# Attention in an audio tower: the order in which a head's six query tiles are worked, 0, 5, 1, 4, 2, 3 in place of 0, 4, 1, 5, 2, 3

## The reference, cut to what matters

```python
q = jnp.einsum('bqd,hdm->bqhm', x, W_Q) + b_Q          # the same for k and v
scores = jnp.einsum('bqhm,bkhm->bhqk', q, k) / jnp.sqrt(jnp.asarray(D_HEAD, q.dtype))
scores = jnp.where(causal[None, None, :, :], scores, jnp.asarray(IGNORE, scores.dtype))
pattern = jax.nn.softmax(scores, axis=-1)
z = jnp.einsum('bhqk,bkhm->bqhm', pattern, v)
attn_out = jnp.einsum('bqhm,hmd->bqd', z, W_O) + b_O
```

## Time and profile before

| | |
|---|---|
| median of 3 runs | 1612.37 us (1612.15, 1612.37, 1617.33) |
| profiled execution, its own time | 1609.28 us |
| its span | 1607.5 us |
| busy: PE, PEld | 88%, 61% |
| busy: DVE, ACT, POOL | 66%, 48%, 25% |
| mean granted clock of TensorE | 0.938 of full |

### The profile page before, as it was taken

How to read it: one execution, slowest core, us unless ns; L and a number is a source line. 1 busy time by engine, 2 the same in 40 slices (tenths; PEclk the granted TensorE clock), 3 DMA queues, 4 the chain that set the end, 5 groups by cost and what they waited for, 6 DMA issues and landing times.

```text
span 1607.5 us, 29299 instructions
## 1 busy us (share of the span) xinstructions
PE 1416.6 (88%) x10191; PEld 978.7 (61%) x10192; DVE 1068.1 (66%) x2482; ACT 778.8 (48%) x1490; POOL 408.2 (25%) x425
## 2 busy tenths in 40 slices
PE   5987799998987799998987799999886899969997
PEld 3333378886433488884443588883433788856665
DVE  4988655557987555568896555659886555664553
ACT  1664355643654456525563565616643666532332
POOL 3000044513000244403000334302000576721222
PEclk8899899998998899997989999989998999979999
DMA  5997033210000122201000223200000643222221
GB/s 135 344 352 247 1 73 74 53 36 31 12 1 0 39 69 50 69 12 42 1 1 1 58 56 73 50 1 30 1 1 1 156 120 87 52 68 55 64 61 32
DMA packets 109553, 104.81 MB, mean 65 GB/s; under 512 B 51772, under 2 KB 99961, under 8 KB 109425
## 3 DMA queue, kind: packets, MB, share of 16 engines
q1 hardware_dynamic: 80210, 54.53, 14.1%
q10 hardware_dynamic: 25744, 39.62, 7.5%
q0 software_dynamic: 3472, 8.97, 1.6%
HBM read 28.78 MB, written 47.40 MB: 47 GB/s over the span
## 4 chain that ended last, share of the span: by engine, by line
PE 49%; DVE 28%; issue 10%; POOL 5%; ACT 4%; DMA 2%; SPq 2%; POOLq 0%; DVEq 0%; ACTq 0%
PE ps L1879 12%; DVE arena L1301 10%; PE ps L1929 8%; PE ps L1859 7%; DVE arena L1299 6%; PE ps L1869 6%; DVE bn L1458 4%; PE ps L1812 4%; PE ps L1973 3%; PE ps L1818 2%; DMA arena<-arena 2%; SPq L573 1%; POOL out L900 1%; ACT arena L1002 1%; POOL arena L797 1%
## 5 line engine op out<-in xcount | busy, mean ns | idle before, releaser
L1929 PE MATMUL ps<-arena,cwt 128*128 128x504 f16 (+2 forms) x1776 | 391.6, 381 | 40.8 <-DVE arena L1299 38.7
L1929 PEld LDWEIGHTS ps<-arena,cwt 128*128 128x128 f16 x1776 | 175.5, 102 | 257.1 <-DVE arena L1299 42.3
L1320 DVE TENSOR_REDUCE nmax<-ps 128x1 f32<-128x128 f32 (+5 forms) x288 | 173.5, 615 | 116.6 <-PE ps L1862 116.6
L1879 PE MATMUL ps<-arena 128*128 128x64 f32 (+2 forms) x2016 | 237.8, 270 | 2.6 <-DVE arena L1328 2.6
L1879 PEld LDWEIGHTS ps<-arena 128*128 128x128 f32 (+2 forms) x2016 | 229.9, 188 | 8.3 <-DVE arena L1328 4.2
L1301 DVE TENSOR_TENSOR arena<-arena 128x1008 f16<-128x1008 f32 (+4 forms) x200 | 227.1, 1136 | 6.9
L980 ACT ACTIVATE arena<-ps,nmax 128x128 f32<-128x128 f32 (+5 forms) x288 | 181.2, 630 | 58.9 <-DVE nmax L1320 56.3
L1328 DVE COPY arena<-ps 128x512 f32<-128x512 f32 (+4 forms) x288 | 152.1, 535 | 70.0 <-PE ps L1869 67.0
L1042 ACT ACTIVATE arena<-ps 128x1008 f32<-128x1008 f32 (+1 forms) x112 | 96.1, 866 | 179.8 <-PE ps L1929 179.8
L1859 PE MATMUL ps<-arena 128*128 128x512 f16 (+6 forms) x780 | 154.5, 310 | 19.2 <-DMA arena<-arena 10.4
L786 POOL TENSOR_TENSOR tmp<-tmp,neg_half 128x1 f32<-128x1 f32 x24 | 13.3, 553 | 545.4 <-DVE tmp L1202 545.4
(11 more groups left out here) (291 smaller groups left out, 2242.6 us busy)
## 6 DMA issues: line engine op xcount, KB each, us to landing
slot_scratch<-empty_slot ACTq DMA_DIRECT2D x1, 38692.5 KB, 119.9
arena<-arena SPq DMA_DIRECT2D x96, 187.5 KB, 3.0
arena<-arena SPq DMA_DIRECT2D x96, 93.8 KB, 2.4
arena<-in_L_ffn_w SPq DMA_DIRECT2D x16, 288.0 KB, 6.7
arena<-in_L_ffn_w SPq DMA_DIRECT2D x8, 576.0 KB, 7.5
arena<-slot_scratch SPq DMA_DIRECT2D x31, 96.5 KB, 1.9
arena<-slot_scratch SPq DMA_DIRECT2D x31, 96.0 KB, 1.9
xa<-in_x POOLq DMA_DIRECT2D x4, 468.8 KB, 4.7
```

Of the source, the lines that this page charges most:

```text
L1320: v.reduce_max(nmax[0:m, k:k + 1], banks_at(("S", p, k))[0:m, 0:128 * i + m], AX.X, negate=True).then_inc(S["smax_done"], 1)
L1879: last = t.matmul(bank_at(BANKS[job][0])[0:m, 0:DH], probt[(STEPS * p + k) % PROBTS][0:kk, c, 0:m], vt[0:kk, c, DH * hh:DH * hh + DH], sta ...
L1929: last = t.matmul(bank(g, k)[:, 0:c * PITCH].rearrange("p (r c) -> p r c", c=PITCH), cwt[layer][:, w, tap, :], parts[x][:, f:f + 2 * c - 1 ...
```

## The change

One constant differs. Step 1 (and 7 of the second head) works on tile 5 and step 3 (and 9) on tile 4, where it was the other way round. The three lists of steps, the sizes in PSUM banks (both tiles take two) and all waits between steps stay as they were.

```diff
-TILE_ORDER = (0, 4, 1, 5, 2, 3)
+TILE_ORDER = (0, 5, 1, 4, 2, 3)
 STEPS = 2 * TT
```

## The result

The changed kernel took 1626.47 us in the median of 5 runs (1618.69 to 1626.69). Five runs of the kernel before, made beside them, had a median of 1613.47 us (1612.15 to 1617.33). The ratio is 1.0061 with a 95% interval of 1.0034 to 1.0089. The prediction was 1614.8 us with a range of 1611.0 to 1618.5, and it gave a slowdown of over 0.3% a chance of 0.14.

What follows compares the result with a forecast made beforehand. PE bounds the half from S12 to Q, the stack's DMA the half from Q to S12. Per recording 0.21 + 0.24 + 0.16 = 0.61 us, four times +2.4: 1612.37 to 1614.8 us, range 1611.0 to 1618.5.

Steps and rivals of the forecast that it cites:

- S9's gain: Score step between Q and S12, 0.11 us shorter; in middle pairs it only lengthens S12's DMA wait, 0.28 to about 0.37.
- The rival in which all cancels: S12's wait is an issue delay following PE, so S9's gain counts: +0.7 us in all, 1613.1; chance 0.13.
- the waits of Q and Z3: Q's wait in the first pair about 1.5 us, from 1.33; Z3's in the last about 0.9, from 0.65.
- signs of being wrong: Middle-pair period below 24.84 us or up over 0.15; low clock appearing after first-pair Q or vanishing after S2.
- The rule on the share of the weight loads: Loads busy 3.23 of 4.00 us, so PE has spare time; middle halves cost nothing, sum +1.5 us.
- S12 to Q: Half of a middle pair bound by PE itself: +0.06 us each, four per recording, +0.24 us.
- PT2's wait for EX2: Rival: longer CA1 delays EX2, PT2 waits; up to 0.08 us in each of 24 pairs, +1.9, 1616.7; chance 0.10.
- The margin of 0.12 us for PT2: With S3 0.11 us shorter, PT2 comes up at 235.19, still 0.12 us after EX2's end at 235.07.
- First pair: Path to Q's wait for EX7 through S3, PT1, S7, MX7 and EX7: +0.21 us, bounds +0.10 and +0.25.
- Last pair: No Q or K, so Z3 waits for CP3 and S9's gain counts: +0.16 us per recording.
- The rival of the slow clock: Q's longer first-pair wait brings low clock, 1.7 us per recording hit; all four +9.2, 1621.6; chance 0.08.
- Nothing outside the attention changes, it is shifted: Stages outside the attention only move in time; no cost was added for them.

Runs made afterwards that it cites:

- K split: High part of K sent to the stacks as soon as made, low part when ready: old order 1609.73 us (0.9979), new order 1614.06 us (0.9983).
- the unneeded matmuls before S2: 8 dummy matmuls in the wait before S2 of each recording's first pair: old order 1610.13 us (0.9964), new order 1613.31 us (0.9972).
- the new order with both: Changed kernel plus K split and the unneeded matmuls before S2: 1610.39 us, ratio 0.9966 to the kernel before.
- the old with both: Kernel before plus K split and the unneeded matmuls before S2: 1608.99 us, ratio 0.9948.
- the shifted kernel: Kernel before, old tile order, plus twelve dummy matmuls between ZT and the output projections of each recording: 1623.38 us, ratio 1.0044.

## Why the prediction was wrong, point by point

**The waits held as a mechanism.** A pair is a loop of two halves. S12 waited for the stack's DMA: its matmul started 135 ns behind the last landing in each of the 20 handovers of every kernel with that transfer, its load's wait went to 0.36 us, Q to S12 stayed at 12.80, and the split of the transfer let S9's gain come out. The rival in which all cancels is ruled out by this: middle pairs cost 0.10 us each. All three signs were right, and the waits of Q and Z3 moved as said. None of the signs of being wrong that the prediction named came up (the median period grew by 0.09 us, less than its 0.15); they all watched the attention, and a good third of the loss lies behind it.

The rule on the share of the weight loads that the prediction took from the Trainium skill (Perfetto Trace Analysis, Identifying the Most-Contended Engine), by which middle pairs would have cost nothing, is not borne out by the traces here.

**The terms were too small.** S12 to Q: forecast +0.06, measured +0.10. Of this 0.05 is PT2's wait for EX2, which had a chance of 0.10 as a rival at up to 0.08. The step that failed there was "EX2 waits for MX2 at that time, not for CA1": that was so before (MX2 to EX2 0.10 us), but the row after shows EX2 right behind CA1. The margin of 0.12 us for PT2 was none, since 0.14 us pass between the end of ACT's accumulator read and the start of the transposes. I had noted that part of it was the semaphore's own way and did not take that off. Z1, which I put at 0 with 0.04 as its upper end, costs 0.04 (1.117 to 1.160 us). Against these two stands an error that helped by luck: S13 and S7 were forecast at +0.11 each and cost 0.09 (0.600 to 0.688 us), so that 0.06 + 0.05 + 0.04 - 0.04 comes to the 0.10. First pair: forecast +0.21 to Q, measured +0.25. Last pair: forecast +0.16, measured +0.26. There Z3 to Z9 takes 9.25 us in both kernels, where the prediction had it 0.07 shorter: S9 gives its 0.09 and Z3 0.04, but Z7 takes 0.04 more, Z9's wait for CP9 0.05, and PT7 and Z5 together 0.04. The measured sum is 0.25 + 4 x 0.102 + 0.26 = 0.92 us per recording, 3.7 in all, where the prediction had 2.4 and 3.1 as its upper end. By the table the middle pairs came out at 1.3 us in place of 1.6; their handovers of K's stack happened to be 0.2 us less late.

**Late transfers were left out.** K's stack for the last pair lands later than the others': in the second recording Q to S12 goes 0.04 us beyond 12.78 before and 0.59 after. That adds 0.8 us over the four recordings: 1.82 of the table less 4 x 0.26. It is part of the difference between the two profiles' rows "issue", 1.4 and 2.1 us. Why they landed later was not tested.

**The clock was priced in the wrong place.** The rival of the slow clock had the right kind, the right price (1.7 us a stretch) and was the rival nearest to the result (1621.6 us), but it stood on Q of the first pair, behind which the clock was full in all 24 recordings, and had a chance of 0.08. "Nothing outside the attention changes, it is shifted" is the sentence that failed: it put the clock behind the attention at nothing without a reason, and by the traces the shift is what moved it. The low stretch behind ZT came in 0.79 of the recordings instead of 0.30, and it cost 1.64 us in the mean of the 25 in which it came: (0.79 - 0.30) x 4 x 1.64 = +3.2 us. The first pairs add 0.9 us of clock ahead of Q, the 0.19 and 1.68 of the table less 4 x 0.25; with the errors of those rows, 0.22 and 0.69, and counts of 5 in 20 against 10 in 24, this term alone could be chance.

Together 3.7 + 0.8 - 0.3 + 3.2 + 0.9 = 8.3 us, of the 9.1 ± 0.8 measured.

**The base was low.** The median of the three runs shown was 1612.37, the profile's own time 1609.28. Over 96 further runs the kernel before had medians of 1615.1 to 1617.6 in the three series. So the level that I built on lay 3 to 5 us too low (1 us against the five runs of the result), and my spread of 1 us for the runs was too small: single runs of it lie between 1608.7 and 1623.2.

**What stays open.** That the low stretch comes by where ZT's end falls on the beat is a reading that 76 recordings bear out, not an experiment: ZT's end was not moved by itself. It fits what the other kernels showed: the new order with K split, and with the unneeded matmuls before S2, ended ZT outside that part and had the stretch in 0 of 4 recordings each, the new order with both had it in 4 of 4, the old with both in 2 of 4. Matmuls put between ZT and TC's end, which would fill that wait, were not tried; those of the shifted kernel came after it. One of its four recordings still had the low stretch, and another had none with ZT's end 1.58 us behind a tick, the one case that lies off, in the one kernel with other work there. Of the 3.5 ± 2.3 us between the attentions 1.6 are left beside the low stretches, within the error. K split and the unneeded matmuls brought the two orders nearer by more than the direct costs they touch (K split can hide 0.09 a pair, not 7 us in all), and the low stretches that they moved are a part of that. Why K's stack lands later in the last pair is open too.

## What to carry to other kernels

- When two tiles swap places, sum the steps on each half of the loop apart, and put a handover's own time (here 0.14 us from ACT to PE) against a margin before taking it for one; a producer that grows ahead of it on its engine takes the rest.
- Search the whole program for places where the clock sometimes falls after a wait, also where nothing is changed, and carry them as a term with a chance: here such a place was worth nearly as much as all moved waits. A change that makes the part ahead of such a place longer can move that chance, even if it alters no wait there. Repeat the profile of the kernel before before building on its level.
- What paid was not the order of tiles but the waits themselves: sending the half that is ready early, and filling a long wait of PE ahead of a dense stretch, 0.5% together.

## What the runs showed of the hardware that was not expected

- One program's executions spread over 15 us, and their time went with the mean granted clock, about 0.48 us less for each 0.001 more over the runs of the kernel before. Its profiles had clocks from 0.918 to 0.944.
- The low stretch behind ZT was 3.4 us each time it fell there, at half rate, 1.4 to 1.7 us lost, or not there at all. It came only when ZT ended 1.49 to 2.80 us behind a tick of the beat on which all changes of the granted clock lay, in 37 of 37 recordings; 39 others, with ZT's end elsewhere, had none. It came behind two waits of 0.50 and 1.19 us with 0.83 us of matmuls between, shorter than the wait of 1.84 us before S2 that I had taken as the measure.
- From the last landing of a stack's transfer to S12's first matmul 135 ns passed, in old and new order alike. The profile called the load's wait there "issue" and not DMA.
- The fp32 products whose weights have 110 columns follow one another in 97 ns, those with 128 columns in 112 ns (1.160 us for tile 5's twelve, 1.117 for tile 4's ten).
